# Two attentions on one core: score passes on row tiles of TensorE, keys spread by transfers

## What is computed

```python
x = L0_attn_x                                   # 4 x 1024 x 128
x = x + _layernorm(attn1(_layernorm(x)))        # causal, with a position bias
x = x + _layernorm(ffn(_layernorm(x)))
# attn1: q, k, v = x @ W + b in 16 heads of 8; scores = q k^T * 8**-0.5
scores = scores + alibi_slopes(H)[:, None, None] * pos      # pos = i - j
scores = jnp.where(causal, scores, -jnp.inf)
out = softmax(scores) @ v ; out @ Wo + bo
# ffn: x = x + _layernorm(attn2(x)) * g + b     (attn2: 16 heads of 8, no mask, no bias)
#      x = x + _layernorm(moe(x)) * g + b       (8 experts, the best 2 of each token)
```

## Time and profile before

| | |
|---|---|
| median of 3 runs | 2292.57 us (2288.94 to 2295.37) |
| span of the profiled execution | 2287.5 us |
| TensorE busy | 2102.9 us, 92% |
| VectorE busy | 1671.8 us, 73% |
| ScalarE busy | 1373.5 us, 60% |
| GpSimd busy | 977.3 us, 43% |
| mean granted TensorE clock | 0.959 |

### The profile page before, as it was taken

The page is one execution under the profiler, slowest core; times in us unless marked ns, Lnnn a source line. Parts: engine busy times, 40 slices in busy tenths (PEclk is TensorE's granted clock), DMA queues, the critical chain, the costliest instruction groups (busy, mean ns, idle before and its releaser), DMA issues. The chain is left out here.

```text
span 2287.5 us, 41083 instructions
## 1 busy us (share of the span) xinstructions
PE 2102.9 (92%) x11100; PEld 1223.1 (53%) x11100; DVE 1671.8 (73%) x3157; ACT 1373.5 (60%) x2647; POOL 977.3 (43%) x744
## 2 busy tenths in 40 slices
PE   5899999999999679999999999999993999999996
PEld 4455555555554534555555555555531666666664
DVE  5766667666672787777777777778822899998986
ACT  4266566666666616666666666666672655555654
POOL 3665464553610355333333333342002466565554
PEclk7799999999999679999999999999996999999998
DMA  2000000000000300000000000000001100000000
GB/s 59 1 2 1 3 1 1 2 2 1 1 1 2 110 0 1 2 1 1 2 1 1 2 1 1 1 1 1 1 1 61 51 19 19 2 19 19 19 10 10
DMA packets 27508, 24.96 MB, mean 11 GB/s; under 512 B 2409, under 2 KB 21110, under 8 KB 27282
## 3 DMA queue, kind: packets, MB, share of 16 engines
q1 hardware_dynamic: 26400, 21.91, 3.2%
q10 hardware_dynamic: 882, 0.36, 0.1%
HBM read 13.87 MB, written 6.29 MB: 9 GB/s over the span
## 5 line engine op out<-in xcount | busy, mean ns | idle before, releaser
L466 DVE TENSOR_REDUCE at_mx<-at_a 128x1 f32<-128x512 f32 (+3 forms) x1632 | 1010.8, 675 | 358.7 <-PE at_a L333 249.5
L415 ACT ACTIVATE at_probs<-at_b 128x512 f32<-128x512 f32 (+3 forms) x1792 | 888.6, 558 | 474.0 <-PE at_b L360 292.7
L333 PE MATMUL at_a<-at_km,at_fq 128*128 128x512 f32 (+1 forms) x1632 | 704.8, 439 | 20.4 <-DVE at_mx L466 9.8
L360 PE MATMUL at_b<-at_fqm,at_km 128*128 128x512 f32 (+3 forms) x1792 | 710.8, 404 | 11.4 <-ACT at_probs L415 7.6
L333 PEld LDWEIGHTS at_a<-at_km,at_fq 128*128 128x128 f32 x1632 | 316.3, 194 | 290.0 <-DVE at_mx L466 224.4
L360 PEld LDWEIGHTS at_b<-at_fqm,at_km 128*128 128x128 f32 x1792 | 339.8, 191 | 205.5 <-ACT at_probs L415 120.3
L378 PE MATMUL at_pv<-at_probs,at_vst 128*32 128x512 f32 (+3 forms) x3584 | 437.9, 561 | 1.5 <-ACT at_probs L415 1.5
L556 POOL TENSOR_TENSOR at_hi<-at_u,split_sign 128x512 fp32r<-128x512 f32 x120 | 124.9, 1041 | 441.1 <-ACT at_u L404 306.5
L1172 ACT ACTIVATE t_hid<-t_bank_h,b1t 128x512 f32<-128x512 f32 x256 | 174.3, 689 | 195.9 <-DVE t_hid_lo L1306 113.1
L1306 DVE TENSOR_TENSOR t_hid_lo<-t_hid,t_hid_hi 128x512 fp32r<-128x512 f32 x256 | 225.6, 917 | 15.0 <-ACT t_hid_hi L1179 11.8
L569 POOL TENSOR_TENSOR at_km<-at_fk,head_mask 128x2048 fp32r<-128x2048 f32 x60 | 216.1, 3602 | 11.2 <-POOL at_fk L567 11.0
(11 more groups left out here) (211 smaller groups left out, 2410.3 us busy)
## 6 DMA issues: line engine op xcount, KB each, us to landing
t_raw<-L_ffn_W SPq DMA_DIRECT2D x16, 256.0 KB, 3.1
x_first<-L_attn_x SPq DMA_DIRECT2D x4, 512.0 KB, 7.3
second_x_in<-L_attn_x SPq DMA_DIRECT2D x8, 256.0 KB, 3.1
kept<-second_joined SPq DMA_DIRECT2D x8, 256.0 KB, 2.6
kept_u<-second_normed SPq DMA_DIRECT2D x8, 256.0 KB, 2.0
t_heads_in<-tokens SPq DMA_DIRECT2D x8, 256.0 KB, 2.6
t_u_in<-kept_u SPq DMA_DIRECT2D x8, 256.0 KB, 3.1
t_x_in<-kept SPq DMA_DIRECT2D x8, 256.0 KB, 3.1
```

The costliest lines, as they stand in the source:

```text
L333: mm = pe.matmul(scores, fq[g][:, qt * P:(qt + 1) * P], km[g][:, heads[0]:heads[0] + k, kh * HALF:kh * HALF + w], start=True, stop=not dia ...
L360: mm = pe.matmul(out[:, 0:w], km[g][:, j, kt * P:(kt + 1) * P], fqm[g % 2][:, q0:q0 + w], start=True, stop=not diagonal)
L415: act.activation(probs[(t % 2) * GH + j][:, 0:w], b_bank[n % 3][:, 0:w], ACT.Exp).then_inc(exp_done, 1)
L466: dve.tensor_reduce(mx[:, kh, qt, heads[0]:heads[0] + k], a_bank[n % 3][:, 0:k * w].rearrange("p (k w) -> p k w", k=k), AX.X, ALU.max).the ...
```

## The change

- The rows of the array are used in tiles. A first-pass matmul takes the 64 rows of two heads, a second-pass one the 32 rows of its head. `km` keeps two copies instead of four, the even and the odd heads' rows, allocated and cleared once ahead of both attentions.
- GpSimd (and VectorE in the first slot) no longer multiplies keys by the head mask. Four transfers from SBUF to SBUF per half of the keys, issued by SyncE, copy each head's 32 rows from `fk` (now two buffers) into `km`. TensorE waits for them, and GpSimd waits for the last slot's ones before it overwrites `fk`.
- Banks: four for the second pass; `misc` is gone, and projections and both kinds of transposes take turns with the first pass in one ring of three banks. `probs` holds four quads instead of two.
- The list: per step first the four `b`, then all `a`, then `pv` and `oev`, then the rest. `b` runs three quads ahead (`lead`), the `pv` of a step is that of quad i+1.
- The chunks of the first pass go in the order of heads 0, 2, 1, 3 and hold at most two heads: 40 in at1. Its diagonal mask is two matmuls of 64 rows each.
- The diagonal of the second pass isn't masked by TensorE any more: GpSimd clears the exponentials of the upper triangle (`affine_select`, eight times per slot of at1).

```diff
+RING = ("a", "proj", "otr", "mtr")
+A_BANKS = 3
+B_BANKS = 4
+PROBS = 4
+KEYS = 16 * GH
+PAIR = 2 * HW
...
-                per = max(1, HALF // n)
-                per = 4 if per >= 4 else per
-                for j in range(0, GH, per):
+                per = 2 if n <= HALF // 2 else 1
+                for j in (0, 2) if per == 2 else (0, 2, 1, 3):
...
-        self.lead = 2
-        a_steps = nq - 4
+        self.lead = 3
+        a_steps = nq - 2 - self.lead
...
-            out += self.interleave(bs, ass)
+            early = len(ass)
+            out += bs + ass[:early]
+            dp, p = (0, i + 1) if i + 1 < self.nq else (1, 0)
+            if dp == 0 or do_a1:
+                out.append(("pv", dp, p))
+                if p in self.half_end:
+                    out.append(("oev", dp, self.half_end.index(p)))
+            out += ass[early:]
...
-                        mm = pe.matmul(scores, fq[g][:, qt * P:(qt + 1) * P],
-                                       km[g][:, heads[0]:heads[0] + k, kh * HALF:kh * HALF + w],
+                        rows = slice(PAIR * (heads[0] // 2), PAIR * (heads[0] // 2 + 1))
+                        first = heads[0] % 2
+                        mm = pe.matmul(scores, fq[g][rows, qt * P:(qt + 1) * P],
+                                       km[g][rows, first:first + k, kh * HALF:kh * HALF + w],
                                        start=True, stop=not diagonal)
                         if diagonal:
-                            mm = pe.matmul(scores[:, :, w - P:w], ident16[:, :],
-                                           causal_mask[:, None, :].broadcast_to([P, k, P]),
-                                           start=False, stop=True)
+                            for i in range(2):
+                                mm = pe.matmul(scores[:, :, w - P:w], half_ident[rows, i, :],
+                                               half_mask[rows, i, None, :].broadcast_to([PAIR, k, P]),
+                                               start=False, stop=(i == 1))
...
-                        mm = pe.matmul(out[:, 0:w], km[g][:, j, kt * P:(kt + 1) * P],
-                                       fqm[g % 2][:, q0:q0 + w], start=True, stop=not diagonal)
-                        if diagonal:
-                            mm = pe.matmul(out[:, 0:P], causal_mask[:, :], ident16[:, :],
-                                           start=False, stop=True)
+                        out = b_bank[n % B_BANKS]
+                        rows = slice(HW * j, HW * (j + 1))
+                        mm = pe.matmul(out[:, 0:w], km[g][rows, j % 2, kt * P:(kt + 1) * P],
+                                       fqm[g % 2][rows, q0:q0 + w], start=True, stop=True)
...
+                    if what == "b" and n % GH == GH - 1 and n // GH in plan.diagonals:
+                        await_(exp_done, NB, s, n)
+                        block_ = probs[n // GH % PROBS][:, :, 0:P]
+                        pool.affine_select(block_, block_, [[0, GH], [1, P]], ALU.is_ge, 0.0, base=0,
+                                           channel_multiplier=-1).then_inc(masked, 1)
...
-                        await_(pool_step, count, s, step + 2)
-                        pool.tensor_tensor(km[g][:, :, half],
-                                           fk[:, None, :].broadcast_to([P, GH, HALF]),
-                                           head_mask[:, :, None].broadcast_to([P, GH, HALF]),
-                                           ALU.mult).then_inc(split_done, 1)
...
+                    for j in range(GH):
+                        rows = slice(HW * j, HW * (j + 1))
+                        sp.dma_start(km[g][rows, j % 2, h * HALF:(h + 1) * HALF].bitcast(F32),
+                                     fk[h][rows, :].bitcast(F32)).then_inc(keys_spread[h], 16)
```

More of the change, by code:

```diff
@@ L76, in __init__ @@
                 self.quads.append((qh, kt))
+        self.diagonals = [t for t, (qh, kt) in enumerate(self.quads) if causal and kt * P >= qh * HALF]
         self.na = len(self.chunks)
@@ L129, in body, with places @@
                 out.append(("mtr", 1, self.mt_steps.index(i)))
-            dp, p = (ds, q - 1) if q else (0, self.nq - 1)
-            if dp == 0 or do_a1:
-                out.append(("pv", dp, p))
-                if p in self.half_end:
-                    out.append(("oev", dp, self.half_end.index(p)))
-        return out
+        return out
+    def places(self, steps):
+        order = [step for step in steps if step[0] in RING]
+        return {step: place for place, step in enumerate(order)}
     def prologue(self):
@@ L234, in attention @@
         rec = sb("rec", [P, HQ, GH])
-        a_bank = [bank(f"a{i}") for i in range(3)]
-        b_bank = [bank(f"b{i}") for i in range(3)]
+        a_bank = [bank(f"a{i}") for i in range(A_BANKS)]
+        b_bank = [bank(f"b{i}") for i in range(B_BANKS)]
         pv_bank = bank("pv")
-        misc = bank("misc")
+        in_body = plan.places(plan.body())
+        in_prologue = plan.places(plan.prologue())
+        assert len(in_body) % A_BANKS == 0
         proj_made = sem("proj_made")
@@ L247, in attention @@
         dve_step = sem("dve_step")
+        keys_spread = [sem(f"keys_spread{i}") for i in range(2)]
         v_staged = sem("v_staged")
@@ L387, in emit @@
                         mm.then_inc(o_turned, 1)
+                if prologue:
+                    done(pe, proj_read, 4, s0 + 2, 3)
+                    done(pe, fqm_made, 2, s0, 1)
+                    done(pe, a_read, NA, s0 + 1, plan.a_next - 1)
             run(pe, emit)
@@ L394, in _, with emit @@
                 act.sem_inc(semaphore, per)
-            def emit(steps, s0, b0, g0):
+            def emit(steps, s0, b0, g0, places, before):
                 for what, ds, n in steps:
@@ L438, in emit @@
                         un = u[n % 2]
-                        own = 5 * h if m else 5 * h + 3
+                        own = 4 * h + 2 * (n % 2)
                         done(dve, proj_read, 4, s, n)
@@ L504, in _ @@
         def _(pool):
-            for semaphore, per in ((split_done, 4), (v_staged, 1)):
-                pool.sem_inc(semaphore, per)
+            for semaphore, per in ((split_done, 4), (v_staged, 1), (masked, len(plan.diagonals))):
+                if per:
+                    pool.sem_inc(semaphore, per)
             pool.memset(mpad[:, :, :], 0.0).then_inc(init, 1)
@@ L1516, in gpsimd @@
                 pool.memset(row3[:, :, :, :, :], 0.0).then_inc(zeroed, 1)
+                for i in range(2):
+                    pool.memset(km[i][:, :, :].bitcast(F32), 0.0).then_inc(cleared, 1)
                 pool.wait_ge(zeroed, 1)
```

166 lines of the change are left out of this document (96 added, 70 removed).

## The result

| | before | after |
|---|---|---|
| median | 2291.41 us (2288.94 to 2295.37, 4 runs) | 2306.72 us (2302.19 to 2315.18, 4 runs) |
| span of the profiled execution | 2287.5 us | 2301.0 us |
| mean granted TensorE clock | 0.959 | 0.916 |
| TensorE busy | 2102.9 us | 2004.0 us |

The ratio is 1.0074, interval 1.0048 to 1.0099: the kernel is 0.7% slower where 2270.6 us was forecast, inside the range of 2150 to 2400 but in the wrong direction. TensorE is busy for 99 us less, and the kernel still takes longer.

What follows compares the result with a forecast made beforehand. TensorE was taken to set the pace; its saved time becomes waiting on the third bank. Terms of -9 - 10 - 3 causal, +6 - 3 - 4 full and +1 gave -22: 2270.6 us, range 2150 to 2400.

Steps and rivals of the forecast that it cites:

- ahead of the loops: Stretches before the two attentions' loops: 10 us shorter in the causal attention, 3 us in the full one.
- the first part: Start of the kernel: the larger mask constant is waited for, +1 us.
- rival (d): Loop steps: TensorE's waits lower its clock to 1.2 GHz; one step in ten there, +90, 2360 us; chance 0.10.
- The step of four chunks: Full attention: the fourth first-pass chunk waits for the first's reduction, so a step takes 3.11 us against 3.05.
- The full slot: Full attention, one head group: 55.0 us against 54.55, +0.4 per slot, +6 for 15 slots.
- The causal slot: Causal attention, one head group: 39.5 us against 40.1, -0.6 per slot, -9 for 15 slots.
- The mask on probabilities: Causal attention: GpSimd clears exponentials eight times per slot, taken as 1.3 us each, for which it has room.
- rival c: Causal attention: from about 2 us per GpSimd mask the value product waits; at 3.6, +85, 2355 us; chance 0.10.
- The keys by transfer: Key copies on SyncE's queue: no cost in the loops, covered by splits ahead; if uncovered, some 3 us twice.
- The last slots: End of each attention, without first-pass chunks: four banks let ScalarE run through, -3 us causal and -4 us full.
- Rival (a): Both attentions' steps: tiles pack better, shape changes and loads hidden, 0.25 less per step, -105, 2165 us; chance 0.22.
- (b): Second-pass group: 32-row loads issued in turn, 0.30 more, +126, 2397 us; without any overlap 2560; chance 0.20.

Runs made afterwards that it cites:

- full_a: Changed kernel with the first score pass and its causal masks over 128 rows instead of 64: 2279.27 us, ratio 0.9954 to the kernel before.
- unroll: Changed kernel with the hardware loop written out for the first three batches of either attention: 2263.34 us, ratio 0.9889 to the kernel before.
- banks2: Changed kernel with two banks instead of three in the ring of the first pass: 3041.46 us in a single run.
- rows_ab: Changed kernel with first and second score pass over all 128 rows, masks kept at 64 rows: 2466.57 us in a single run.

## Why the prediction was wrong

Its sum was 35.5 us too low (+13.5 for -22). By the stage table the two stretches ahead of the loops account for 23.5 + 17.4 = 40.9 of that. The 12 + 12 slots account for -18.9 + 26.4 = 7.5. The rest of the attentions gave 8.8 + 7.3 = 16.1 more than was forecast, the first part took 3 more, the other two stages 0.2. 40.9 + 7.5 - 16.1 + 3 + 0.2 = 35.5.

**The clock is the step that failed.** The sum has no term for it: ahead of the loops it takes 10 and 3 us off as if the clock stayed as it was. The clock stands only in rival (d), as short waits inside full stretches, with a chance of 0.10. In the full attention's loop the clock does hold (0.98 in the window; beside the turns, two dips of 3 us). It fails where something interrupts TensorE. Ahead of both loops, where 10 and 3 us were to be won, 13 and 15 were lost; of the 40.9 us that this part was off, full_a takes back 31 (16.9 and 14.2), and for the other 10 there is no experiment. At the two causal turns a slot has 13 us more than its neighbours, 3.5 before, so 9.5 twice = 19 us; at the two full ones 6.7 and 5.4 more instead of 3.9 and 4.3; and two other full slots with a dip have 1.2 each. full_a shows that the form of the first pass, 64 rows or 128, decides most of how long the clock stays down ahead of the loops and part of it at the turns; unroll shows that the turns are one of the triggers. The earlier trace rows had the drop; the prediction read it as a price for emptiness, and didn't ask how long the return takes with another shape. Without the 19 us of the turns, the 12 causal slots would stand at 12 x (36.9 - 40.6) = -44 rather than -26. The Trainium skill, "TensorE: Matmul & The Clock Gate", A second HAM failure mode: psum-queue depth-cycling, describes a clock that swings where TensorE idles shortly between groups of matmuls; banks2 agrees with it, at 0.64 and 0.70 in the loops with two banks in the ring. The prediction named that rule and took this kernel's waits to be too short for it, which holds for the full loop with three banks (0.98); it is not what happened ahead of the full loop, where TensorE is busy 99% and 96%.

**The step of four chunks was right**: 3.13 for 3.11, released by the reduction of the first chunk, as the timeline above shows. Other lengths read from the same timelines: five chunks 3.73 (3.71), three 2.09 (2.07), a projection 0.89 (0.88), the second-pass group 0.43 (0.42). The Trainium skill's 3.07 times for four row tiles ("TensorE: Matmul & The Clock Gate", Measured speedup vs the span model), by which the group would have taken 0.09 more, doesn't hold here: the prediction's 0.21 within the group fits the measured 0.43, the four loads start within 0.01 us of each other, and a group of 256 columns takes 0.32 (510.05 to 510.37), so that 256 columns more cost the four together 0.11, what one matmul needs for them.

**The full slot was 1.2 too short** (56.2 for 55.0), and this is a missing term. The transposes of the maxima now stand in the ring of three banks. Timeline after, behind a block of first-pass chunks:

```profile
1483.65 1.89 DVE L499 TENSOR_REDUCE at_mx<-at_a 128x1 f32<-128x512 f32 x3
1484.47 0.42 PEld L382 LDWEIGHTS at_a<-ident,at_mpad 128*128 128x128 f32 x4 [1.86 <-DVE at_mpad L514]
1484.48 0.65 PE L382 MATMUL at_a<-ident,at_mpad 128*128 128x128 f32 x4 [0.96 <-DVE at_mx L499]
```

They wait 0.96 for a reduction to give a bank back; before they had one of their own. The bare sum of the prediction was 54.6; with 1.0 for this wait and 15 steps at 0.02 more it is 55.9, and 0.3 of the measured 56.2 stays open (the prediction's unexplained 0.4 covered that, and not the wait). Twelve slots and their turns and dips: +31 for +4.8.

**The causal slot was 2.6 too long** (36.9 for 39.5), also a matter of size: the price of two chunks with masks. TensorE in a step on the diagonal, after:

```profile
505.38 0.40 PE L219 MATMUL at_a<-turned_hi,w_lo 128*128 x1
505.71 0.39 PE L352 MATMUL at_a<-iota_rows,slope_rows 6*128 6x512 bf16 x1
505.71 0.55 PE L396 MATMUL at_b<-at_fqm,km 32*128 32x384 f32 x4
506.20 0.51 PE L368 MATMUL at_a<-km,at_fq 64*128 64x512 f32 x2
506.54 0.29 PE L373 MATMUL at_a<-half_mask,half_ident 64*128 64x128 bf16 x4
506.95 0.49 PE L368 MATMUL at_a<-km,at_fq 64*128 64x512 f32 x1
...
507.61 0.50 PE L368 MATMUL at_a<-km,at_fq 64*128 64x512 f32 x1
```

Two chunks of different heads and their four half masks take 0.75 together (506.20 to 506.95) where the prediction had 2 x (0.23 + 0.30) = 1.06: heads 0 and 2 lie in different halves of the rows, so their tiles run side by side. The prediction counted that for the 32-row tiles and not for these. And the 6-row matmul of the positions starts with the second pass (both 505.71), so a projection with it takes 0.90 instead of 1.11. In this slot projections come to 3.6 (4.0 forecast), transposes to 2.3 (2.5), the steps themselves to 31.0 (33.0). This is the largest thing that went better: over 12 slots -44 us for -7.

**The mask on probabilities** (rival c) was priced too high. Groups by line, after (busy us, mean ns, idle before):

```profile
L580 POOL TENSOR_SCALAR_AFFINE_SELECT at_probs<-at_probs 128x512 f32<-128x512 f32 x128 | 80.6, 635 | 197.5 <-ACT at_probs L455 197.5
...
L413 PE MATMUL at_pv<-at_probs,at_vst 128*32 128x512 f32 (+3 forms) x3584 | 454.8, 581 | 1.1 <-POOL at_probs L580 1.1
```

0.635 us, not 1.3, and the product's matmuls waited 1.1 us for it in the whole run.

**The keys by transfer** cost nothing that shows: DMA issues of the page, after (KB each, us to landing):

```profile
km<-at_fk SPq DMA_DIRECT2D x256, 64.0 KB, 2.0
```

VectorE has its four splits done by 63.9 us and goes straight on to reductions, as was forecast. What that won ahead of the loops was eaten by the clock: VectorE waits 1.6 to 2.5 us for first-pass matmuls again and again up to 91 us, and the clock is at 0.50 from 70 to 91.

**The last slots** gave 8.8 and 7.3 us more than forecast, and **the first part** took 3 more. GpSimd waits for the larger mask constant there until 14.4, only 0.7 later than for the smaller one before (13.7), so the forecast's 1 was enough for it. TensorE's clock is low from 28 to 59 us, before from 26 to 39 and again from 46; neither part was taken apart by an experiment.

**Rival (a)**, all steps packed better, is wrong for the full attention and partly right for the causal one; **(b)** is ruled out by the group at 1202.07 and by rows_ab. **(d)** did not happen in its place, the short waits of full stretches; the clock's cost came at the loops' beginnings and turns.

## What to carry to other kernels

Price what a smaller tile does outside its steady state: count the places where TensorE stops (ahead of a loop, at its turn), and read for each how long the clock stays down and which matmuls bring it back. A form that is shorter in every undisturbed slot (36.9 for 38.3, 56.2 for 56.55) was slower in all by 1.2%. And when matmuls get cheaper, place the long one that needs no bank between those that do: with three banks for VectorE, the product in the middle, after the larger half of the chunks, gave 79 us together (2279.3 to 2200.3).

## What the runs showed of the hardware

- Granted clock and rows. With 64-row first-pass matmuls TensorE was 99% and 96% busy at the 1.2 GHz level in two windows of 20 us, and stayed there for 27 us at each causal turn and 82 ahead of a loop; with 128-row ones in the same program for 14 and 7 us at the turns, and 7 and 10 ahead of that loop.
- Two banks instead of three in the ring, first pass on 64 rows: clock 0.64 and 0.70 in the loops where three give 0.94 and 0.98.
- Four 32-row matmuls of 512 columns in four banks: 0.43 from the first load to the load behind them. Two 64-row ones with their masks: 0.75 against 0.66 for one alone.
- Changing between heights: a 128-row matmul of 512 columns, followed by 64-row masks, takes 0.43 until the mask starts, 0.23 where another 128-row one follows; the chunk with its masks takes 0.65, and 0.43 where the masks have 128 rows too.
- A turn of the hardware loop stops TensorE for 2.8 us before and 3.0 after the change; written out, the loop has no such pause and the slots there are as long as the others.
